# Turning the gathered rows of a mixture of experts by transposing DMAs instead of on TensorE

## The reference

```python
scores = einsum(q, k) / 16 * layernorm(x); masked;  p = softmax(scores)      # 4 x 1024 x 1024
x = x + tanh(g_xattn) * p
h = layernorm(x).reshape(4096, 1024)
w, sel = top_k(softmax(h @ gate_w.T), 8);  w = w / sum(w)
# each expert takes its first CAP = 256 tokens, xin[e]: 256 x 1024
act = silu(xin[e] @ wg[e]) * (xin[e] @ wu[e])                                # 256 x 384
y[token] += w * (act @ wd[e])                                                # 256 x 1024
x = x + tanh(g_ffn) * y
```

## Time and profile before

| | |
|---|---|
| median of 3 runs | 2090.3 us (2084.61 to 2091.12) |
| span of the profiled execution | 2089.3 us, 37900 instructions |
| TensorE busy, granted clock | 1924.5 us (92%), mean clock 0.962 |
| DVE, ACT, POOL busy | 1313.1 us (63%), 1143.8 us (55%), 811.9 us (39%) |
| DMA | 501.27 MB, 240 GB/s over the span |

### The profile page before, as it was taken

How to read it: one execution, slowest core, us unless ns; L and a number is a source line. 1 busy time by engine, 2 the same in 40 slices (tenths; PEclk the granted TensorE clock), 3 DMA queues, 4 the chain that set the end, 5 groups by cost and what they waited for, 6 DMA issues and landing times.

```text
span 2089.3 us, 37900 instructions
## 1 busy us (share of the span) xinstructions
PE 1924.5 (92%) x13696; PEld 1429.0 (68%) x13760; DVE 1313.1 (63%) x2221; ACT 1143.8 (55%) x1507; POOL 811.9 (39%) x751
## 2 busy tenths in 40 slices
PE   7777777529999999999999999999999999999998
PEld 3444444427777777777777777777777777777775
DVE  5766666536666666666666666666666666666663
ACT  5555555425555555555555555555555555555553
POOL 0788788762323332333232333322222322332321
PEclk9999997659999999999999999999999999999999
DMA  5465443227888888888888888888888888888883
GB/s 219 150 237 185 134 137 134 94 77 248 272 275 276 279 277 279 276 278 276 264 264 267 270 266 270 275 276 278 278 278 278 278 278 266 264 266 269 267 269 74
DMA packets 90632, 501.27 MB, mean 240 GB/s; under 512 B 17761, under 2 KB 19553, under 8 KB 65505
## 3 DMA queue, kind: packets, MB, share of 16 engines
q1 hardware_dynamic: 45536, 362.24, 43.7%
q0 software_dynamic: 45056, 138.58, 29.9%
HBM read 396.69 MB, written 104.07 MB: 240 GB/s over the span
## 4 chain that ended last, share of the span: by engine, by line
PE 78%; POOL 11%; issue 8%; DMA 1%; POOLq 0%; DVE 0%; ACT 0%; SPq 0%; DVEq 0%
PE ps_gu L454 48%; PE ps_d L463 24%; POOL place_table L923 10%; PE ps_x L439 5%; POOL norm L916 1%; PE ps_j L369 0%; PE ps_s L380 0%; DMA b_qk<-in_bqT 0%; PE ps_t L369 0%; DMA xg<-h_rows,g_idx 0%; POOLq L923 0%; DMA place_table<-token_no,where 0%; POOLq L94 0%; DMA table<-place_table 0%; DVE xb L792 0%
## 5 line engine op out<-in xcount | busy, mean ns | idle before, releaser
L980 POOL DMA_INDIRECT out<-ob,s_idx x128 | 207.2, 1619 | 1051.5 <-ACT ob L632 1029.8
L454 PE MATMUL ps_gu<-xT,split_g 128*128 128x256 bf16 x4608 | 536.2, 273 | 0.0
L454 PE MATMUL ps_gu<-xT,split_u 128*128 128x256 bf16 x4608 | 534.4, 273 | 0.0
L463 PE MATMUL ps_d<-split_d,act 128*128 128x512 bf16 x2240 | 493.9, 379 | 3.4
L454 PEld LDWEIGHTS ps_gu<-xT,split_g 128*128 128x128 bf16 x4608 | 451.9, 98 | 65.1
L454 PEld LDWEIGHTS ps_gu<-xT,split_u 128*128 128x128 bf16 x4608 | 450.9, 98 | 52.2
L838 DVE TENSOR_TENSOR split_d<-raw_d,split_d 128x1536 bf16<-128x1536 f32 x128 | 219.3, 1755 | 398.6 <-ACT split_d L615 398.6
L463 PEld LDWEIGHTS ps_d<-split_d,act 128*128 128x128 bf16 x2304 | 225.4, 98 | 258.2
L923 POOL DMA_INDIRECT place_table<-token_no,where x256 | 294.0, 1148 | 77.6 <-issue 77.3
L619 ACT ACTIVATE sil<-ps_gu 128x256 f32<-128x256 f32 x192 | 73.7, 384 | 445.3 <-PE ps_gu L454 445.3
L632 ACT ACTIVATE ob<-ps_d,wcol 128x512 f32<-128x512 f32 x256 | 171.3, 687 | 259.0 <-PE ps_d L463 259.0
(11 more groups left out here) (86 smaller groups left out, 1426.0 us busy)
## 6 DMA issues: line engine op xcount, KB each, us to landing
raw_g<-in_wg SPq DMA_DIRECT2D x64, 1536.0 KB, 11.6
raw_u<-in_wu SPq DMA_DIRECT2D x64, 1536.0 KB, 15.7
raw_d<-in_wd SPq DMA_DIRECT2D x64, 1536.0 KB
h_rows<-hrow SPq DMA_DIRECT2D x34, 544.0 KB, 3.6
xb<-in_x SPq DMA_DIRECT2D x32, 512.0 KB, 5.0
out<-xb SPq DMA_DIRECT2D x32, 512.0 KB, 2.7
ctx_sb<-in_ctxT SPq DMA_DIRECT2D x4, 1024.0 KB, 8.7
place_table<-token_no,where POOLq DMA_INDIRECT x256
```

Of the source, the lines that this page charges most:

```text
L454: mm = pe.matmul(ps_gu[m][:, t, :], w[:, wi, k, m * P:(m + 1) * P], xT[u][:, k, xi, :], start=(k == 0 and (wi, xi) == (0, 0)), stop=(k == ...
L463: mm = pe.matmul(ps_d[n % 3][:], act[u][:, ai, m, half * P:(half + 1) * P], split_d[:, wi, m, c * NH:(c + 1) * NH], start=(m == 0 and (wi, ...
L980: p.indirect_dma_start(out=out, out_offset=bass.IndirectOffsetOnAxis(ap=s_idx[u][:, half:half + 1].bitcast(U32), axis=0), in_=ob[u][:, hal ...
```

## The change

The gathered rows aren't turned by TensorE any more. ACT copies the 1024 features of each half of xg into the high part of a new tile xs (one buffer, bf16) and DVE subtracts to get the low part beside it; these two copies and two subtractions stand at the head of each expert's order on both engines, and for expert 0 ahead of the splits of its weights. SP then issues two DMAs for each expert that transpose from SBUF to SBUF, one for each half of 128 rows: each takes xs[:, half], 128 partitions x 2048 bf16 (512 KB), into xT. SP issues them between raw_d for e + 1 and raw_g, raw_u for e + 2. TensorE waits for both (`turned`) before an expert's first matmul. xT's layout changes so that high and low are its outer dimension. The freed PSUM banks give ps_d a fourth. POOL's gather waits for the low parts instead of the transposes.

```diff
-        xT = [sb(f"xT{u}", [P, KH, 2, CAP], BF16) for u in range(2)]
+        xs = sb("xs", [P, 2, 2, H], BF16)
+        xT = [sb(f"xT{u}", [P, 2, KH, CAP], BF16) for u in range(2)]
...
-        ps_x = [ps(f"ps_x{i}", [P, 2, CAP], F32, ctx) for i in range(2)]
-        ps_d = [ps(f"ps_d{i}", [P, NH], F32, ctx) for i in range(3)]
+        ps_d = [ps(f"ps_d{i}", [P, NH], F32, ctx) for i in range(4)]
...
+            def turn(u):
+                for half in range(2):
+                    sp.dma_start_transpose(xT[u][:].rearrange("p a k c -> p (a k) c")[:, :, half * P:(half + 1) * P],
+                                           xs[:, half].rearrange("p a h -> p (a h)")).then_inc(turned[u], 16)
+
             def expert(e, u, ahead):
 
                 if ahead >= 1:
                     sp.wait_ge(d_low, 2 * e + 2)
                     load_down(e + 1)
+                    turn(1 - u)
                 if ahead >= 2:
                     sp.wait_ge(g_low, 2 * e + 2)
                     sp.wait_ge(u_low, 2 * e + 2)
                     load_expert(e + 2, u)
 
+            sp.wait_ge(rows_low, 2)
+            turn(0)
...
-                        if m == 0 and t == 0 and k % 2 == 0:
-                            pe.wait_ge(xT_out, 4 * e + k // 2 + 1)
+                        if m == 0 and t == 0 and k == 0:
+                            pe.wait_ge(turned[u], 16 * (e - u) + 32)
                         for wi, xi in PAIRS:
-                            mm = pe.matmul(ps_gu[m][:, t, :], w[:, wi, k, m * P:(m + 1) * P], xT[u][:, k, xi, :],
+                            mm = pe.matmul(ps_gu[m][:, t, :], w[:, wi, k, m * P:(m + 1) * P], xT[u][:, xi, k, :],
...
-                    if m < 2 and not last:
-                        turn(e + 1, 1 - u, 2 * m)
-                        turn(e + 1, 1 - u, 2 * m + 1)
                 down(e, u, first)
...
-            def turned_high(e, u, q):
-                s.wait_ge(xT_done, 4 * e + q + 1)
-                s.activation(xT[u][:, 2 * q:2 * q + 2, 0], ps_x[q % 2][:], ACT.Copy).then_inc(xT_high, 1)
+            def high_rows(e, u, half, first=False):
+                s.wait_ge(gathered[u], 16 * (e - u) + 32)
+                if not first:
+                    s.wait_ge(turned[1 - u], 16 * (e - u) + 32 * u)
+                s.activation(xs[:, half, 0], xg[u][:, half, 0:H], ACT.Copy).then_inc(rows_high, 1)
...
             def expert(e, u, first=False, last=False):
 
                 none_before = first and u == 0
+                if not last:
+                    high_rows(e + 1, 1 - u, 0)
+                    high_rows(e + 1, 1 - u, 1)
                 down_high(e, 0, none_before)
                 down_high(e, 1, none_before)
                 silu(e, 0)
                 if not last:
-                    turned_high(e + 1, 1 - u, 0)
-                    turned_high(e + 1, 1 - u, 1)
                     gate_high(e + 1, 1 - u, 0, none_before)
                     gate_high(e + 1, 1 - u, 1, none_before)
...
+            def low_rows(e, u, half):
+                v.wait_ge(rows_high, 2 * e + half + 1)
+                v.tensor_tensor(xs[:, half, 1], xg[u][:, half, 0:H], xs[:, half, 0], ALU.subtract).then_inc(rows_low, 1)
...
                 if ahead >= 2:
-                    p.wait_ge(xT_done, 4 * e + 4)
+                    p.wait_ge(rows_low, 2 * e + 2)
                     p.wait_ge(wcol_ready, e + 1)
                     gather(e + 2, u)
```

More of the change, by code:

```diff
@@ L221, in flamingo_moe @@
         wcol_ready = sem("wcol_ready")
-        xT_done = sem("xT_done")
-        xT_high = sem("xT_high")
-        xT_out = sem("xT_out")
+        rows_high = sem("rows_high")
+        rows_low = sem("rows_low")
+        turned = [sem(f"turned{u}") for u in range(2)]
         gu_done = sem("gu_done")
@@ L428, in _ @@
                     project(g // TB + 1, g % TB)
[L431 to L440, removed]
             PAIRS = ((0, 0), (0, 1), (1, 0))
@@ L462, in down_part @@
                     for wi, ai in PAIRS:
-                        mm = pe.matmul(ps_d[n % 3][:], act[u][:, ai, m, half * P:(half + 1) * P],
+                        mm = pe.matmul(ps_d[n][:], act[u][:, ai, m, half * P:(half + 1) * P],
                                        split_d[:, wi, m, c * NH:(c + 1) * NH],
@@ L480, in down, with expert @@
                     down_part(u, n, [MI - 1]).then_inc(down_done, 1)
[L481 to L487, removed]
+                for n in range(2, 4):
+                    if not first:
+                        pe.wait_ge(down_out, 4 * e - 3 + n)
+                    down_part(u, n, range(MI)).then_inc(down_done, 1)
+            def expert(e, u, first=False):
                 for m in range(MI):
                     gate_up(e, u, m, first)
-                    if m < 2 and not last:
-                        turn(e + 1, 1 - u, 2 * m)
-                        turn(e + 1, 1 - u, 2 * m + 1)
                 down(e, u, first)
             attention_done(pe)
-            for q in range(4):
-                turn(0, 0, q, True)
             expert(0, 0, True)
@@ L501, in _ @@
                 expert(2 * i + 2, 0)
-            expert(E - 1, 1, False, True)
+            expert(E - 1, 1)
         @block.scalar
@@ L631, in rows_out @@
                     s.wait_ge(down_done, 4 * e + n + 1)
-                    s.activation(ob[u][:, n // 2, n % 2 * NH:(n % 2 + 1) * NH], ps_d[n % 3][:], ACT.Copy,
+                    s.activation(ob[u][:, n // 2, n % 2 * NH:(n % 2 + 1) * NH], ps_d[n][:], ACT.Copy,
                                  scale=wcol[u][:, n // 2:n // 2 + 1]).then_inc(down_out, 1)
@@ L848, in activate @@
                 v.tensor_tensor(act[u][:, 1, m], prod[:, m], act[u][:, 0, m], ALU.subtract).then_inc(act_ready, 1)
[L850 to L853, removed]
+            def low_rows(e, u, half):
+                v.wait_ge(rows_high, 2 * e + half + 1)
+                v.tensor_tensor(xs[:, half, 1], xg[u][:, half, 0:H], xs[:, half, 0], ALU.subtract).then_inc(rows_low, 1)
             def expert(e, u, first=False, last=False):
+                if not last:
+                    low_rows(e + 1, 1 - u, 0)
+                    low_rows(e + 1, 1 - u, 1)
                 down_low(e, 0)
```

17 lines of the change are left out of this document (6 added, 11 removed).

## The result

The changed kernel takes 2037.99 us in the median (2031.88 to 2041.92, 4 runs) against 2090.56 us: a ratio of 0.9747, with a 95% interval from 0.9724 to 0.9769. It is 53 us faster. The forecast was 2233 us, slower; rival (a) named 2030 us at X = 3.

A forecast was written before the change was run, and what follows sets the result against it. The prediction took TensorE (25.24 us an expert) as the present bound and the DMA engines as the next, at 21.2 + 6.2 = 27.4 us. 2089.3 + 136 + 7 = 2232, given as 2233 us; range 2000 to 2700, own case 2138 to 2335.

The forecast's parts named there:

- rival (a): Transposes at nearly the plain rate, X 2.5 to 3.9: 1997 to about 2084 us, 2030 at X = 3; chance 0.37.
- X: Time of the 16 DMA engines for one expert's 1.05 MB of transposes, set at 6.2 us.
- 21.2 + X (the DMA engines): Expert's DMA time: 84.1% share of 25.24 us plus the transposes, 21.2 + 6.2 = 27.4 us, the bound; +136 us.
- The estimate by the DMAs that handle rows: X as the middle of 4.7 us (whole software queue's rate) and 7.8 us (scatter-add alone) for 1.05 MB: 6.2.
- TensorE's 113 us: Gain from removing 16 transposes in each of 63 experts, 63 x 1.80 us, if nothing else binds; 23.44 us an expert.
- ACT and DVE: Evictions removed (2.4 and 2.7 us an expert), row copies added (2.0 and 2.3 us): no effect on the time.
- The place of the turn and the loop: Turn issued 8.6 us into the expert; loop from one landing to the next, 7.7 + T, 21.4 us, not binding.
- T: Time from a turn's issue to its landing: 5.8 us behind raw_d, 6.2 of transposes, 1.7 of landing.
- The start: Expert 0's rows are turned in the open, by row copies, transposes and landing before its first matmul: +7 us.
- The sign that was to tell the two apart: Expert period: 27.4 us for the main case; 23.4 to 25 with no TensorE idle means (a) holds.
- (b): X just at 4.0, DMA eating all of TensorE's gain: within 6 us of now; chance 0.06.
- (c): Transposes run block by block, 32 each waiting for the last: 68 us an expert, about 4830 us; with slow tail 0.13.

The follow-up runs named there:

- before_plus_turn: Kernel before, TensorE's transposes kept, plus two unread transposing DMAs an expert behind raw_d's load: 2093.56 us, ratio 1.0012.
- double_turn: Changed kernel plus two more transposing DMAs an expert, from a constant tile into an unread scratch tile: 2589.87 us, ratio 1.2406.
- turn_no_scatter: Changed kernel with the scatter-adds left out (POOL copies one column instead): 1980.4 us, ratio 0.947.
- no_turn_dma: Changed kernel with both transposing DMAs of each expert left out, xT holding a constant: 1990.7 us, ratio 0.9516.

## Why the prediction was wrong

**The step that failed** is "21.2 + X (the DMA engines)", a sum of busy shares taken as time. It made two claims, and both are off.

First, that 84.1% leaves 4.0 us of an expert, so that X = 4.0 decides between faster and slower. In before_plus_turn a whole turn, 5.0 us when alone, goes into 25.24 us without a trace. With the measured X in its place the sum would still have said 21.2 + 5.0 = 26.2 and about 2157 us, slower. From 27.4 forecast to 24.33 measured the way is, in the sum's own terms: X by share is 5.3 and not 6.2 (0.9 us); the software queue's share is 35.0% of 24.33 = 8.5 us and not 9.6 (1.1); and the 25.4 us of share that are left go into 24.33 (1.1), because the total runs at 104.5%. So the size of X is less than a third of the error.

Second, that once DMA is full more work costs its own time. It costs 8.9 us a turn. The measured period, 15.4 + 8.9 n, has a lower foot and a steeper slope than 21.2 + 6.2 n, and at n = 1 it is 24.3 where the sum said 27.4. (The foot is where the line points; no run lies below one turn with DMA binding.)

What a share counts is time in which an engine has a packet under way. That this time contains waiting which another queue's packets can fill is the reading of these numbers, not something that a run shows by itself. It fits that the software queue's 9.6 us an expert became 8.5 in before_plus_turn, and that the total went to 1.04 to 1.08. But the shares don't follow a rule that one could add up by: the software queue is back at 28.5% of 33.3 = 9.5 us in double_turn, and the hardware queue's share less 11.6 gives X = 5.3 in the changed kernel, 5.9 in before_plus_turn, 7.7 in turn_no_scatter (82.0% of 23.49) and 7.5 a turn in double_turn. Why a turn beside the other queue costs 8.9 and not 5.0, no run takes apart further than this: without the scatter-adds two turns take 6.2 us less. In double_turn 72.7% of the page's chain is SP's issue of transposes (SPq L351 43.4%, SPq L346 29.3%), and the foot of 15.4 is near the 15.3 us that theory Q gave to the weights on SP's queue. So that queue, rather than the engines behind it, isn't excluded as the part that is full.

**X** was set at 6.2 between bounds of 2.5 and 95; it is 5.0 alone (208 GB/s), and the share in the loop gives no single value. The estimate by the DMAs that handle rows was 24% above 5.0. The rule of the Trainium skill, Advanced Engine Details and Errata, section X-Bar Transpose (TRN2), as fast as regular DMAs, isn't what this trace shows: 208 against 423 GB/s, and at expert 0 5.6 against 2.6 us of the engines for the same bytes. The 261 GB/s of the Trainium skill, DMA: Bandwidth & Descriptors, section Latency and other measured facts, is nearer. The 1309 ns a block of the Trainium skill, VectorE: DVE Perf Modes, section The three transpose paths, is no price for a long transfer: here 32 blocks take 5.0 us.

**TensorE's 113 us.** Right in the price: 23.49 us without transposes, and the floor of 1984 us is 108 us under the kernel before, although its start is 3.5 us longer (466.46 - 448.52 = 17.9 us from the load of the table to the first matmul, 14.4 in the kernel before). The change kept half of it. The other half is 2037.6 - 1982.1 = 55.5 us in the profiled executions: 3.5 are the start, and 62 x (24.33 - 23.49) = 52 the loop. There 74.3 - 43.4 = 31 us are waits for xT, and about 11 are the slow clock behind the six longest of them (last section); the rest, small gaps, isn't taken apart.

**ACT and DVE** at nothing: right. The copies take 1047 and 1222 ns (0.99 and 1.17 us forecast), and no_turn_dma, which keeps the copies, is at the floor.

**The place of the turn and the loop.** Issue 8.6 us into the expert was forecast, 7.6 measured; 7.7 us from a landing to the next issue, 7.3 and 7.6 measured. T was put at 5.8 + 6.2 + 1.7 = 13.7 us and is 17.0 in the expert shown (14.43 of issue and 2.6), so the loop is at 24.6 there and not at 21.4. The term that was too small is the 5.8 us ahead of the turn: it counted raw_d alone, and raw_d takes 11.0 us to land in the median; in the expert shown 6.4 us of raw_u were still ahead of it. The prediction let raw_g and raw_u move back behind the turn and gave them room; raw_g's issue moved from 6.5 us into the expert to 22.3, and their drain came to lie ahead of the next turn. Still, moving the turn ahead made another load late, so this backlog is how a full DMA shows, more than a cause beside it.

**The start.** +7 us forecast; from the load of the table to the first matmul it was 464.43 - 450.02 = 14.4 us (the SP row at 450.02 us of before) and is 469.61 - 447.97 = 21.6: +7.2. Right.

**The rivals.** (a) has the outcome: DMA binding a little above TensorE's time, and faster. Its mechanism is not what happened, and its 2030 us were luck. It wanted transposes nearly as fast as plain rows, X = 3, and X is 5; the sum was too high by about as much. The sign that was to tell the two apart couldn't: read by the sum, a period of 24.33 says X = 24.33 - 21.2 = 3.1. (b) falls with the ratio of 0.9747. (c) is excluded by expert 0, whose two DMAs are issued in 4.69 us.

## What to carry to other kernels

A DMA share of 84% that includes indirect transfers wasn't 84% of a capacity here: try the added traffic by itself, unread, in the kernel as it is, before summing shares. Once DMA was full, an added transfer cost more than its time alone (8.9 us for 5.0). Where DMA binds by less than 1 us an expert (here 24.33 against 23.49), giving back a small part of the work to the engine that has just been relieved can be enough: an eighth of the turn won 36 us. When each order of the queue that is tried makes some other transfer late, look for less work and not for a better order.

## What was not expected of the hardware

The issue of transposing DMAs holds SP for long: 4.69 us for two with an empty queue, 12.5 to 15.5 us behind raw_d from 1000 to 1500 us. The loads behind it are issued that much later. A plain DMA's issue takes 0.34 us in the rows above.

A wait of TensorE of under 3 us can cost more than itself. Ahead of 1056.05 us it waits 2.65 us for xT, and the windows view of the changed kernel then shows the clock at 1.2 of 2.4 GHz:

```profile
1056.05:1057.50 1.45, 1.45 (x7) 1.01 (x8) 0.33 (x1) 1.42 (x2) 0.68 (x2) 0.50 1.13 345
1057.50:1059.00 1.50, 1.50 (x9) 1.03 (x7) 1.50 (x2) 1.50 (x2) 1.42 (x1) 0.50 1.02 382
1059.00:1062.00 3.00, 3.00 (x28) 2.63 (x27) 3.00 (x3) 1.83 (x2) 2.69 (x2) 0.95 1.03 339
```

That expert's 144 gate/up matmuls take 17.45 us instead of 15.72. The same follows each of the six waits of 2.65 to 2.90 us in the loop (17.45 to 17.56 us); after the shorter waits of 0.43 and 0.77 us in the timeline above the clock stays at 1.00 and nothing is added. The three experts behind a slow one start without a wait, then come several with short or no waits, then the next slow one. That the 1.7 us give the DMA engines time to catch up fits this pattern; no run tests it.
